# Zero-padded copies of y and of the softmax weights as moving operands: one matmul for four images in a MetaFormer block

## The reference

```
y   = layernorm(x) over the last axis (j)
scores[n,i,h,j] = sum_c (Wq y)[n,c,i,j] (Wk y)[n,c,h,j] / d
weight = softmax over j of scores + Gq*(q . rq) + Gk*(k . rk)
out = einsum('nihj,nchj->ncij', weight, Gv1 * Wv y) + einsum('nihj,chi->ncij', weight, Gv2 * rv)
x2  = x + out
t   = layernorm(x2) ; Wx = batchnorm(t W^T) over all tokens
ys  = scan over the 1024 tokens of an image: y_t = sigmoid(Wx_t + y_{t-1} V^T)
result = x2 + ys
```

## Time and profile before

| what | value |
|---|---|
| time, median of 3 runs | 182.66 us (181.72 to 184.68) |
| profiled execution, device time | 181.89 us |
| its span, first to last instruction | 180.1 us |
| busy: PE, PE weight loads, DVE, ACT, POOL | 120.9, 79.4, 93.1, 65.8, 61.3 us |
| mean granted TensorE clock | 0.816 of 2.4 GHz |

### The profile page before, as it was taken

The page is one execution under the profiler, slowest core; times in us unless marked ns, Lnnn a source line. Parts: engine busy times, 40 slices in busy tenths (PEclk is TensorE's granted clock), DMA queues, the critical chain, the costliest instruction groups (busy, mean ns, idle before and its releaser), DMA issues.

```text
span 180.1 us, 7348 instructions
## 1 busy us (share of the span) xinstructions
PE 120.9 (67%) x3390; PEld 79.4 (44%) x3390; DVE 93.1 (52%) x152; ACT 65.8 (37%) x156; POOL 61.3 (34%) x66
## 2 busy tenths in 40 slices
PE   0067879459956977367648875986876377999800
PEld 0032546454556460357542162665431114799700
DVE  1507852717510509700330299732279765987993
ACT  0217605851720042202201463413132424899900
POOL 4610477042640303612750028357224200000870
PEclk9999978975996596557955897599699955899995
DMA  5970000000000000000000000000000000000257
GB/s 149 319 189 2 4 4 4 4 4 5 4 4 7 4 4 0 4 4 4 9 4 0 4 4 4 5 4 4 4 0 0 0 0 0 4 0 0 84 166 217
DMA packets 6763, 5.53 MB, mean 31 GB/s; under 512 B 1805, under 2 KB 5901, under 8 KB 6733
## 3 DMA queue, kind: packets, MB, share of 16 engines
q1 hardware_dynamic: 6084, 4.77, 9.2%
q10 hardware_dynamic: 648, 0.30, 0.7%
HBM read 2.97 MB, written 2.10 MB: 28 GB/s over the span
## 4 chain that ended last, share of the span: by engine, by line
PE 44%; DVE 21%; issue 16%; ACT 11%; DMA 5%; ACTq 2%
PE ps L908 9%; PE ps L918 8%; PE ps L969 7%; PE ps L895 6%; PE ps L940 6%; PE ps L980 5%; DMA gates<-in_L_conv_Gk_dram 5%; ACT warm L585 4%; DVE xin L286 3%; DVE y L292 2%; PE ps L875 2%; DVE stat L706 2%; DVE u_tile L724 2%; ACT yt_tile L585 2%; DVE stat L694 2%
## 5 line engine op out<-in xcount | busy, mean ns | idle before, releaser
L969 PE MATMUL ps<-att,yt_tile 32*32 32x32 f32 x1024 | 16.8, 229 | 13.2 <-issue 10.6
L908 PE MATMUL ps<-y,u_tile 32*32 32x32 f32 x1024 | 17.3, 230 | 10.1 <-issue 9.4
L969 PEld LDWEIGHTS ps<-att,yt_tile 32*32 32x32 f32 x1024 | 15.4, 130 | 18.5 <-issue 18.5
L908 PEld LDWEIGHTS ps<-y,u_tile 32*32 32x32 f32 x1024 | 16.4, 143 | 12.8 <-issue 11.2
L980 PE MATMUL ps<-u_tile,w_bd 128*128 128x512 f32 x16 | 12.8, 906 | 6.7 <-DVE u_tile L724 6.7
L334 POOL TENSOR_TENSOR att<-att,soft 128x1024 f32<-128x1024 f32 x4 | 7.6, 1912 | 26.9 <-DVE soft L663 26.9
L689 DVE TENSOR_TENSOR x<-ps,x 128x512 f32<-128x512 f32 x8 | 5.4, 675 | 20.6 <-POOL x L356 20.6
L292 POOL TENSOR_TENSOR y<-xin,x 128x256 f32<-128x256 f32 (+1 forms) x7 | 7.1, 1044 | 25.8 <-DVE xin L286 25.8
L658 DVE TENSOR_TENSOR att<-ps,bias_tile 128x1024 f32<-128x1024 f32 x4 | 4.9, 1224 | 20.6 <-PE ps L908 19.8
L366 POOL TENSOR_TENSOR x2n<-x2n,stat 128x512 f32<-128x512 f32 x7 | 7.3, 1047 | 22.9 <-DVE stat L711 22.9
L940 PE MATMUL ps<-y,wv 32*32 32x512 f32 x64 | 14.5, 1032 | 0.0
(11 more groups left out here) (91 smaller groups left out, 213.0 us busy)
## 6 DMA issues: line engine op xcount, KB each, us to landing
out_dram<-y SPq DMA_DIRECT2D x8, 256.0 KB, 2.4
xin<-in_x_dram SPq DMA_DIRECT2D x3, 512.0 KB, 7.6
xin<-in_x_dram SPq DMA_DIRECT2D x2, 256.0 KB, 3.1
rv_in<-in_L_conv_rv_dram SPq DMA_DIRECT2D x4, 128.0 KB, 3.1
r_in<-in_L_conv_rq_dram ACTq DMA_DIRECT2D x1, 128.0 KB, 6.7
r_in<-in_L_conv_rk_dram ACTq DMA_DIRECT2D x1, 128.0 KB, 8.8
gates<-in_L_conv_Gv_dram SPq DMA_DIRECT2D x2, 0.5 KB, 6.5
wsmall<-in_L_conv_Wk_dram ACTq DMA_DIRECT2D x1, 16.0 KB
```

Source lines behind the costliest of these rows:

```text
L908: ins = nc.tensor.matmul(ps[p, SCORE_BANK[q] + jh, C * (j % 16):C * (j % 16 + 1)], u[p, q, :, j], y[p, q, :, j], start=True, stop=True)
L969: ins = nc.tensor.matmul(ps[p, WSUM_BANK[q] + jh, C * (j % 16):C * (j % 16 + 1)], v_t[p, q, j, :], att[p, q, :, j], start=True, stop=True)
```

## The change

A tile spread4 of 128 partitions by 16,384 columns (8 MB) is added. It is set to zero in four quarters at the start (DVE, ACT, POOL, POOL). Then 16 DMAs from SBUF to SBUF (spread_y) copy y so that for each q the block of group g stands on its own 32 partitions at its own columns and is zero elsewhere; a matmul with 128 rows, the 32 columns of u of all four g as weights and such a moving operand does the four images of one q, whose result lands on the 32 PSUM partitions q. The columns now are (g, i). Scores are computed in halves of i: half A for all q (64 moving columns: 4 g by 16 i), then half B, and the softmax works on four chunks of (half, pair of g). Later 16 DMAs (spread_att) write the softmax weights into the same tile, padded in the same way, with g and q exchanged, for the relative values and the weighted sums. The values come from y as weights and a block-diagonal Wv as the moving operand, so they need no transpose; x is added by a matmul with an identity (same) into the same PSUM bank. The loads of Wk, Wq, rq, rk and two gates move to SyncE's queue; the first two centrings move to VectorE.

Counts of the program's matmuls: scores 512 to 256 (64 columns), relative scores 256 to 128 (128 columns), values 32 to 128 (128 columns), relative values 256 to 128 (128 columns) and 8 of a full 128x128 with 512 columns, weighted sums 512 to 256 (64 columns). The scan and the batch norm are unchanged.

The diff, cut to its core; of TensorE's functions only the new lines stand, the old ones are in the kernel above:

```
+        spread4 = sb("spread4", [P, CHUNKS, G, IMG])
...
+        y_bd = spread4[:, :, :, :].rearrange("p q g (i j) -> p q g i j", j=C)
+        att_bd = spread4[:, :, :, :].rearrange("p x q (g i j) -> p x q g i j", g=2, j=C)
...
-        SCORE_BANK = [2, 4, 2, 4]
-        WSUM_BANK = [0, 2, 0, 4]
-        REL_BANK = [6, 7]
-        WX_BANK = [2, 3]
+        SCORE_A, SCORE_B = 2, 0
+        SIDE = [6, 7]
+        R_BANK = 0
+        WSUM_BANK = [2, 0]
+        WX_BANK = [4, 5]
+        VALUES_EARLY = 4
...
+            def spread_y(q):
+                wait_y(sp, q)
+                sp.wait_ge(S[f"spread_zero{q}"], 1)
+                for g in range(G):
+                    sp.dma_start(spread4[group(g), q, g, :], y[group(g), q, :, :].rearrange("p i j -> p (i j)")
+                                 ).then_inc(S[f"y_in{q}"], 16)
+            def spread_att(n):
+                sp.wait_ge(S["weights"], n + 1)
+                sp.wait_ge(S["rel_product"], PIECES4)
+                sp.wait_ge(S["score_b_high"], 1)
+                for q in range(Q):
+                    sp.dma_start(spread4[group(q), n, q, :], att_tile[group(q), IMG * n:IMG * (n + 1)]
+                                 ).then_inc(S[f"att_in{n}"], 16)
+            load_x(0)
+            load_x(1)
+            load_small(3, Wk, "wqk_in")
+            load_small(4, Wq, "wqk_in")
+            load_x(2)
+            load_x(3)
+            load_x(4)
...
+            spread_y(0)
+            spread_y(1)
             for g in range(G):
                 sp.dma_start(rv_in[group(g), :], rv.rearrange("c h i -> c (h i)")).then_inc(S["rv_in"], 16)
+            spread_y(2)
+            spread_y(3)
             for k, a in enumerate((gamma, beta)):
                 sp.dma_start(affine[:, k:k + 1], bass.AP(a.tensor, 0, [[0, G], [1, C], [1, 1]])).then_inc(S["affine_in"], 16)
+            spread_att(0)
+            spread_att(1)
+            spread_att(2)
+            spread_att(3)
...
+            nc.gpsimd.memset(spread4[:, 2, :, :], 0.0).then_inc(S["spread_zero2"], 1)
+            pool.wait_ge(S["ln_mean"], 3)
+            ln_centre(nc.gpsimd, 2, "ln_centred")
+            pool.wait_ge(S["ln_mean"], 4)
+            ln_centre(nc.gpsimd, 3, "ln_centred")
+            nc.gpsimd.memset(spread4[:, 3, 0:1, :], 0.0).then_inc(S["zeros"], 1)
+            pool.wait_ge(S["ln_mean"], 5)
+            ln_centre(nc.gpsimd, 4, "ln_centred")
+            pool.wait_ge(S["ln_rstd"], POOL_SCALED + 1)
+            pool.wait_ge(S["ln_squared"], POOL_SCALED + 1)
+            ln_scale(nc.gpsimd, POOL_SCALED, "y_ready_pool")
+            nc.gpsimd.memset(spread4[:, 3, 1:4, :], 0.0).then_inc(S["spread_zero3"], 1)
...
-            add_input(0)
-            add_input(1)
-            add_input(2)
-            add_input(3)
...
+            act.wait_ge(S["nought_set"], 1)
+            nc.scalar.copy(spread4[:, 1, :, :], nought[:, 0:1].unsqueeze(2).broadcast_to([P, G, IMG])
+                           ).then_inc(S["spread_zero1"], 1)
...
-            ln_square(0)
-            ln_square(1)
             ln_std(0)
             ln_std(1)
-            act.wait_ge(S["r_product"], 1)
-            nc.scalar.mul(r_fac[:, :, :], ps[:, 6:8, :].rearrange("p b (h i) -> p i (b h)", i=C), 1.0 / d
-                          ).then_inc(S["r_ready"], 1)
             ln_square(2)
             u_half(0, 0)
             u_half(0, 1)
             ln_std(2)
             ln_square(3)
+            spread_out(0, 4)
+            spread_out(1, 3)
             ln_std(3)
+            ln_square(4)
             u_half(1, 0)
             u_half(1, 1)
-            ln_square(4)
-            rel_out(0)
             ln_std(4)
...
             u_half(3, 1)
+            act.wait_ge(S["rv_in"], 16 * G)
+            nc.scalar.mul(rv_s, rv_in.rearrange("p (h i) -> p i h", h=C), gates[:, 3:4]).then_inc(S["rv_scaled"], 1)
+            for n in range(VALUES_EARLY):
+                value_out(n)
+            rel_out(0)
+            rel_out(1)
+            rel_out(2)
+            rel_out(3)
+            rel_out(4)
+            rel_out(5)
+            rel_out(6)
+            score_exp(0)
+            rel_out(7)
             score_exp(1)
-            for n in range(PARTS, 2 * PARTS):
-                rel_out(n)
+            for n in range(VALUES_EARLY, PIECES4):
+                value_out(n)
             score_exp(2)
-            value_out(0)
-            value_out(1)
-            value_out(2)
-            value_out(3)
             score_exp(3)
             relv_out(0)
             relv_out(1)
             relv_out(2)
             relv_out(3)
...
             t_square(0)
             t_std(0)
             t_square(1)
             t_std(1)
+            relv_out(4)
             t_square(2)
             t_std(2)
+            relv_out(5)
             t_square(3)
-            wx_out(0)
             t_std(3)
-            wx_out(1)
-            relv_out(4)
-            relv_out(5)
-            wx_out(2)
             relv_out(6)
             relv_out(7)
-            wx_out(3)
+            wx_out(0)
+            wx_out(1)
...
+            nc.vector.memset(spread4[:, 0, :, :], 0.0).then_inc(S["spread_zero0"], 1)
...
+            def score_max(n):
+                first = SCORE_A if n < 2 else SCORE_B
+                if n < 2:
+                    dve.wait_ge(S["score_a"], 1)
+                else:
+                    dve.wait_ge(S["score_b_low"], 1)
+                    dve.wait_ge(S["score_b_high"], 1)
+                dve.wait_ge(S["rel_ready"], 4 * (n // 2 + 1))
+                gs = slice(2 * (n % 2), 2 * (n % 2) + 2)
...
             residual(0)
             residual(1)
-            turn_values(2)
-            turn_values(3)
+            residual(2)
             t_sum2(0)
-            residual(2)
+            residual(3)
             t_rstd(0)
             t_sum2(1)
             t_rstd(1)
-            residual(3)
+            t_sum2(2)
             t_turn(0)
-            t_sum2(2)
             t_rstd(2)
-            t_turn(1)
             t_sum2(3)
             t_rstd(3)
+            t_turn(1)
+            residual(4)
+            t_turn(2)
+            residual(5)
+            t_turn(3)
             bn_part(0)
-            t_turn(2)
-            t_turn(3)
+            residual(6)
+            t_sum2(4)
             bn_part(1)
-            residual(4)
-            residual(5)
-            bn_part(2)
-            bn_part(3)
-            t_sum2(4)
             t_rstd(4)
+            residual(7)
...
+            def score(half, j, q):
+                first = SCORE_B if half else SCORE_A
+                at = G * HALF * (j % 8)
+                return nc.tensor.matmul(ps[group(q), first + j // 8, at:at + G * HALF].rearrange("p (g i) -> p g i", g=G),
+                                        u[:, q, :, j], y_bd[:, q, :, HALF * half:HALF * (half + 1), j], start=True, stop=True)
+            def scores_a(qs):
+                for q in qs:
+                    pe.wait_ge(S["u_half"], 2 * q + 2)
+                    pe.wait_ge(S[f"y_in{q}"], 16 * G)
+                for j in range(C):
+                    for q in qs:
+                        ins = score(0, j, q)
+                return ins
+            def relative_scores(n):
+                if n < 2:
+                    pe.wait_ge(S["value_ready"], VALUES_EARLY - 1 + n)
+                else:
+                    pe.wait_ge(S["rel_ready"], n - 1)
+                for k in range(ROWS):
+                    for q in range(Q):
+                        ins = nc.tensor.matmul(side_bank(n)[group(q), P * k:P * (k + 1)].rearrange("p (g j) -> p g j", g=G),
+                                               r_fac[:, ROWS * n + k, :], y_bd[:, q, :, ROWS * n + k, :], start=True, stop=True)
+                ins.then_inc(S["rel_product"], 1)
+            def project_values(n):
+                pe.wait_ge(S["w_set"], G)
+                if n < 2:
+                    pe.wait_ge(S["u_half"], 2 * (Q - 1) + n + 1)
+                elif n < VALUES_EARLY:
+                    pe.wait_ge(S["value_ready"], n - 1)
+                elif n < VALUES_EARLY + 2:
+                    pe.wait_ge(S["rel_ready"], PIECES4 - 1 + n - VALUES_EARLY)
+                else:
+                    pe.wait_ge(S["value_ready"], n - 1)
+                for k in range(ROWS):
+                    for q in range(Q):
+                        ins = nc.tensor.matmul(side_bank(n)[group(q), P * k:P * (k + 1)], y[:, q, :, ROWS * n + k],
+                                               w_bd[:, 0, :], start=True, stop=True)
+                ins.then_inc(S["value_product"], 1)
+            def relative_values(n):
+                half, row = n // 4, ROWS * (n % 4)
+                if n < 2:
+                    pe.wait_ge(S["value_ready"], PIECES4 - 1 + n)
+                else:
+                    pe.wait_ge(S["relv_ready"], n - 1)
+                nc.tensor.matmul(side_bank(n).rearrange("p (i q j) -> p i q j", i=ROWS, q=Q), same[:, :],
```

(86 more changed lines are left out.)

363 lines of the change are left out of this document (136 added, 227 removed).

## The result

The changed kernel takes 190.5 us (median of 4, 189.9 to 191.7) against 183.6 for the kernel before beside it: a ratio of 1.047, 95% interval 1.036 to 1.057. It is slower; 166 was forecast. The profiled execution has a span of 189.9 us and took 191.72.

A forecast was written before the change was run, and what follows sets the result against it. TensorE's instruction supply was taken as the bound, 58.3 ns per program matmul, with 936 matmuls instead of 1600. Last weighted sum 108.7, plus 24.5, 30.9 and 1.8, gave 166 us; range 153 to 179.

The forecast's parts named there:

- What bounds the kernel before: TensorE's instruction supply: 256 instructions per 3.73 us, 58.3 ns per program matmul; array and clock don't set it.
- The price of a 64-column matmul instruction in column tiles: Scores and weighted sums: at the high clock 53 ns alone, 13 four at a time, below the supply.
- B low and high: Scores of half B, first and last 16 j, four q alternating in column tiles: 3.7 us each.
- Column tiles beside each other: New matmuls on all 128 rows: four column tiles run at once, so instruction supply still sets 58.3 ns per program matmul.
- the serial rival: Column tiles don't overlap, TensorE is the bound throughout: 226 us; chance 0.15.
- The sign that I had named for the serial rival: Where four q alternate, 64-column matmuls 53 ns apart, 107 per program matmul.
- The start: Before the scores: y of q=0 at 12.9, of q=1 at 17.6, u of both until 19.5; DVE's zeroing 4.3 us.
- The clock: TensorE from 19.5: 58.7 at full clock, 66 at low clock throughout; a third of the 27 us between taken, until 68.
- The copies: spread_y and spread_att DMAs: 3.1 us to landing; spread_y hidden, TensorE idle 3 us for spread_att.
- The rival with 10 us more: Copies hold the instruction packets or each other, 8 to 12 us in all: 176 us; chance 0.14.
- Relative values 4 to 7 held by ScalarE's order: relv_out(4), (6), (7) stand behind t_std; relative values 7 end 12.7 us after weighted sums A.
- The tail: Last weighted sum to end of aggregate 24.5 us (bounds 21, 28), then 30.9 as before.

The follow-up runs named there:

- e6: Kernel before, with weights and moving operands of its scores and weighted sums contiguous instead of at 128-byte steps (times only): 181.7 us, ratio 0.996.
- e1: Changed kernel, with the scores' moving operand in runs of 16 neighbours instead of columns 128 bytes apart (times only): 173.0 us, ratio 0.947 to the kernel before.
- e4: Changed kernel, with moving operands of scores and weighted sums and the scores' weights all contiguous (times only): 160.9 us, ratio 0.881 to the kernel before.
- e9: Changed kernel, same result, with rows of 33 elements instead of 32, so moving columns lie 132 bytes apart: median 179.5 us beside 184.2 for the kernel before.
- e3: Kernel of e2, with weighted sums at steps of 8, 16, 64 bytes and in pairs, scores B low reading neighbours (times only): 172.9 us, one run.
- e7: Changed kernel, with ScalarE's relv_out(4) to (7) moved ahead of t_square(0): 183.1 us, ratio 0.995 to the kernel before.
- e11: Changed kernel, with scores A of all four q interleaved behind the early values: 181.1 us, ratio 0.975 to the kernel before.
- e2: Changed kernel, same result, with the scores' weights contiguous (u written in the order j, h): 186.3 us, ratio 1.016 to the kernel before.

## Why the prediction was wrong

*What bounds the kernel before*: right. e6 took 0.7 us out of a burst and the time moved by 0.4%, no more than the interval allows for no change.

*The price of a 64-column matmul instruction in column tiles* is the step that failed. I priced it from contiguous full matmuls (53 ns alone, 13 four at a time, so hidden under 29.1 of supply), and took the old bursts' 15.7 ns, the same at either clock, as proof that array and clock don't matter. The step of the operands had no term in the sum. That burst was set by it: in runs (e6) it takes 1.27 us instead of 2.0 at the full clock, and 1.93 at half. The rows already spoke against the 13 ns: they had 15.7 for an instruction of 32 columns, and I put one of 64 below it. 15.7 ns with four tiles at once is 63 ns in each tile for 32 columns. With twice the columns it is 113 to 120 ns in a lone tile, and a round of four such at 128-byte steps takes 176 to 206 together. The terms that this mis-sized, forecast against measured: q=0 and q=1 alone 3.4 each, 7.4; two q 3.7, 8.9; B low and high 3.7 each, 6.4; weighted sums 7.5 each, 11.3. Together 26.2 us. e1 and e4 confirm it: without the steps 17.5 and 29.6 us go.

The Trainium skill (SBUF — State Buffer, in the note on "cachelines" under Door 1) has the rule that I left out: a line is 16 bytes, and reads that take less than two elements of a line run slower. The trace agrees in part: steps of 16 and 64 bytes take 30 ns, against 15 to 16 in runs; but steps of 8 bytes (18 ns) and pairs (24) take two elements of a line and are slower than runs all the same. The rule names no larger step, and in the runs 128 and 256 bytes are dearer than 132 to 192. Priced by the rows of e9 (a lone q 7.7 us, two q 7.5, four 3.9, weighted sums 7.7), gaps but no hindrance between tiles, the sum would have been 13 us higher: 179 us as an estimate, 2% under the kernel before.

*Column tiles beside each other*: right, the serial rival (0.15) is out. 128 columns at 28 to 30 ns are four tiles at once (107 alone). The kernel did become slower, for which I had 0.15, but by a mechanism that none of the rivals had. The sign that I had named for the serial rival, 64-column instructions 53 ns apart where four q alternate, came true with 50 to 52, and by chance: e3 has the same instructions at 15 ns in runs. The sign could not tell serial tiles from slow reads. The rule of the Trainium skill (TensorE: Matmul & The Clock Gate, Part 3) that loads overlap only with other rows disagrees with the trace again: in e3 four tiles on the same rows, each instruction with its own load, took 15 ns each, where a lone tile took 59 (e4).

*The start*: y of q=0 at 13.07 (12.9 forecast), DVE's zeroing 3.5 us (4.3). But TensorE was at 0.58 and 0.55 for u(0) and u(1), 3.3 each instead of 1.9: 22.2 instead of 19.5. Part of it is y of q=1, ready at 18.9 and not at 17.6.

*The clock*: a third of the way to the low level was taken, 9 us by the end of values 7; nothing of it came from 22.2 on, where the mean clock was 1.00 until 80.9. The sum was wrong there in the other direction.

*The copies*: 2.3 to 2.4 us to landing (3.1 forecast), 0.86 of issue each with the wait (13.7 us for 16); TensorE waited 4.2 us for them, 3 forecast. The rival with 10 us more did not come true: the scores beside the copies of y (22.20) took the 7.4 us of those without (33.31).

*Relative values 4 to 7 held by ScalarE's order*: right in kind, 15.3 us for 12.7; e7 gets 7 back.

*The tail*: from 133.87 (122.58 + 11.29) to 158.62 is 24.8 us, 24.5 forecast; then 31.3, 30.9 forecast.

*The last weighted sum*: 108.7 forecast, 133.9 measured. 26.2 for the strided terms, 2.7 the start, 2.7 relative values 4 to 7, 0.9 relative values 0 to 3, 1.2 more of idle, less 9 for the clock, makes 24.7 of the 25.2. In the sum itself, the start of relative scores was a little off: by the terms given, relative scores 3 end at 43.9 and not at 44.6.

## What to carry to other kernels

Before many small matmuls are made into fewer wide ones, write down for each operand how far apart neighbouring columns lie, and price it from a row of the same step. A group that is fed too slowly hides such a price, and the change that cures the feeding uncovers it. A row pitch of 128 or 256 bytes is to be suspected where several tiles of the array read all partitions: one spare element per row gave back 7 us in the weighted sums here. And issue tiles that differ in their columns interleaved, not one tile's matmuls in a row: 23.7 us of scores A became 12.9 (e11). Last, name a sign for a rival that no other rival would give too.

## What the hardware did that I had not expected

The price of a matmul instruction with 64 float32 columns and 128 rows, by the step of its moving operand and at full clock, from the runs above:

```
step            one tile   four tiles, per instruction (supply 29)
4 bytes (runs)  59 ns      15 to 17  (24 to 25 with weights at 128 bytes; one tile 61)
8 bytes         -          18
pairs           -          24
16, 64 bytes    -          29 to 30
32 bytes        -          31
132 bytes       120        30 to 31
144             -          30
160, 192        -          31 to 32
128 bytes       113        44 to 45  (50 to 52 with weights at 128 bytes; one tile 116)
256 bytes       -          59
```

From 16 bytes on, apart from 128 and 256, the column for four tiles is the rate of the supply or just above it.

The other engines felt it. In the changed kernel VectorE's sum of scores and ScalarE's exponential took 1502 and 1419 ns on average, where they took 1224 and 1058 before. With either the moving operand (e1) or the weights (e2) of the scores in runs they are back at 1202 to 1219 and about 1080, and with rows of 33 (e9), weights still at 128 bytes, at 1204 and 1086. The means hide when: in the changed kernel, the instructions beside scores B (60.53 to 66.95 and 70.56 to 76.92) are slow, and those behind them are not:

```profile
61.74 1.80 DVE L690 TENSOR_TENSOR att_tile<-ps,rel_tile 128x1024 f32<-128x1024 f32 x1 [15.00 <-ACT rel_tile L466]
...
77.63 1.16 DVE L690 TENSOR_TENSOR att_tile<-ps,rel_tile 128x1024 f32<-128x1024 f32 x1
```

```profile
71.83 1.72 ACT L471 ACTIVATE att_tile<-att_tile 128x1024 f32<-128x1024 f32 x1
...
82.09 1.06 ACT L471 ACTIVATE att_tile<-att_tile 128x1024 f32<-128x1024 f32 x1 [0.55 <-POOL att_tile L378]
```

Which part of the memory the streams meet in is not settled: the runs show the dependence on the step and on the number of tiles, and no more.
